# A scheduled attention and FFN kernel: new stage positions, a new VectorE order, and the residual added in one operation

## What is computed

```python
x = x + ln(attention(ln(x), Wq, Wkv, Wo, bo))                  # 32 heads of 16, 8 groups, causal
x = x + ln(ffn0(ln(x)))      # 1792 wide: silu(x gate^T) * (x up^T), then down^T, ternary weights with scales
x = x + ln(lags(ln(x)))      # autocorrelation of each row by FFT, 6 largest lags, softmax of their values,
                             # sum of the row rolled by these lags with these weights
x = x + ln(ffn1(ln(x)))      # 1376 wide, the same form, weights w + b a (rank 16)
```

## Time and profile before

| | us |
|---|---|
| median of 3 runs (lowest 926.63, highest 937.12) | 927.11 |
| the profiled execution, whole | 937.81 |
| its span from the first to the last instruction | 936.0 |
| TensorE busy, all of the span | 755.1 |
| VectorE busy, all of the span | 650.8 |

### The profile page before, as it was taken

How to read it: one execution, slowest core, us unless ns; L and a number is a source line. 1 busy time by engine, 2 the same in 40 slices (tenths; PEclk the granted TensorE clock), 3 DMA queues, 4 the chain that set the end, 5 groups by cost and what they waited for, 6 DMA issues and landing times. The chain is left out here.

```text
span 936.0 us, 15978 instructions
## 1 busy us (share of the span) xinstructions
PE 755.1 (81%) x5102; PEld 409.0 (44%) x5102; DVE 650.8 (70%) x1681; ACT 363.5 (39%) x699; POOL 290.2 (31%) x348
## 2 busy tenths in 40 slices
PE   1966765979898898989859986869974899979995
PEld 1622211222222232222326654646742677757773
DVE  7522874766776767786789977577999954797422
ACT  1112223544565555676003332536431354323221
POOL 3023443112022120233104553334551432533332
PEclk9977755989999998998888997989987999989998
DMA  9499789781231231546556412120229420110100
GB/s 268 82 149 320 232 237 228 148 178 40 43 63 27 48 62 36 136 109 217 175 132 144 83 35 84 62 46 25 61 55 144 85 57 1 23 23 23 46 23 24
DMA packets 144333, 93.12 MB, mean 99 GB/s; under 512 B 111816, under 2 KB 123208, under 8 KB 144056
## 3 DMA queue, kind: packets, MB, share of 16 engines
q1 hardware_dynamic: 133216, 69.93, 33.2%
q10 hardware_dynamic: 10816, 16.91, 6.2%
q0 software_dynamic: 240, 5.51, 2.8%
HBM read 48.20 MB, written 29.04 MB: 83 GB/s over the span
## 5 line engine op out<-in xcount | busy, mean ns | idle before, releaser
L1126 PE MATMUL ps<-arena 128*128 128x256 f16 (+1 forms) x1952 | 236.6, 278 | 26.4 <-issue 13.9
L1126 PEld LDWEIGHTS ps<-arena 128*128 128x128 f16 (+1 forms) x1952 | 195.7, 101 | 70.5 <-issue 24.0
L1353 ACT ACTIVATE arena<-ps 128x1024 f32<-128x1024 f32 (+7 forms) x256 | 163.7, 651 | 124.1 <-PE ps L1383 119.6
L1374 PE MATMUL ps<-arena 96*128 (+4 forms) x384 | 136.8, 382 | 41.8 <-DVE mx L1290 14.2
L1286 DVE CUSTOM_DVE_ANT_0 arena<-ps,arena 128x256 bf16<-128x256 f32 (+3 forms) x256 | 122.2, 489 | 59.0 <-PE ps L1374 50.9
L980 POOL TENSOR_TENSOR arena<-arena 128x256 f32<-128x256 f32 (+1 forms) x100 | 81.2, 812 | 243.2 <-ACT arena L871 241.9
L1148 PE MATMUL ps<-arena 128*128 128x512 f16 (+2 forms) x488 | 123.4, 383 | 17.9 <-POOL arena L986 17.6
L1383 PE MATMUL ps<-arena 99*128 (+4 forms) x384 | 128.3, 352 | 4.7 <-ACT arena L1353 4.3
L1261 POOL TENSOR_SCALAR_AFFINE_SELECT arena<-arena 128x512 f32<-128x512 f32 x64 | 42.1, 659 | 230.6 <-ACT arena L1353 230.3
L1290 DVE TENSOR_REDUCE mx<-ps 128x1 f32<-128x512 f32 x128 | 88.3, 689 | 35.0 <-PE ps L1374 34.2
L1374 PEld LDWEIGHTS ps<-arena 96*128 (+1 forms) x384 | 39.5, 103 | 151.3 <-issue 82.1
(11 more groups left out here) (154 smaller groups left out, 843.0 us busy)
## 6 DMA issues: line engine op xcount, KB each, us to landing
arena<-qp_d SPq DMA_DIRECT2D x48, 128.0 KB, 4.2
lora_d<-arena ACTq DMA_DIRECT2D x20, 256.0 KB, 4.6
arena<-lora_d SPq DMA_DIRECT2D x10, 512.0 KB, 4.8
w1n_d<-arena SPq DMA_DIRECT2D x10, 512.0 KB, 3.3
arena<-rec_d SPq DMA_DIRECT2D x32, 128.0 KB, 2.6
qp_d<-arena SPq DMA_DIRECT2D x12, 256.0 KB, 4.1
w1dn_d<-arena SPq DMA_DIRECT2D x4, 704.0 KB, 3.9
arena<-in_L_ffn_down_w_dram ACTq DMA_DIRECT2D x16, 172.0 KB, 3.7
```

The lines of the kernel that those rows point to most:

```text
L1126: last = nc.tensor.matmul(ps[0:h, b, CH * o:CH * (o + 1)], w(t[0])[:, kt, ht * P:ht * P + h], xt[:, c, t[1], kt, :], start=(kt, t) == (0, ...
L1353: nc.scalar.activation(probs[:, kt % 2, h, kt * P:T], st_bank(h).rearrange("p b n -> p (b n)")[:, kt * P:T], ACT.Exp, scale=HD ** -0.5).th ...
L1374: nc.tensor.matmul(s_bank(g, u)[:, 0:k1 - k0], qt6[0:QROWS, g % RING, h, qt * P:(qt + 1) * P], kt6[0:QROWS, g, k0:k1], start=True, stop=Tr ...
```

## The change

Four things are changed.

1. **The norm.** The first norm's result is no longer written out and added. One `scalar_tensor_tensor` for each tile adds y * rstd to x; the mean that is left out is kept in `shift` for each row, and the last norm adds it. (A norm of x does not see a constant added to a row.) The Newton steps of a 2-column rsqrt are done column by column, two operations for each column and step, without a wait between the columns.
2. **Positions.** The tables become `ROWS_AT` (26, 45, 64, 76), `CORR_AT` (28, 49, 65, 77), `LAGS_AT` (30, 53, 66, 78), `SPEC_AT` (39, 59, 71, 82), `PROD_AT` (43, 61, 73, 84), `BACK_AT` (47, 62, 74, 86). They were (23, 36, 59, 66), (26, 39, 61, 68), (28, 41, 63, 70), (38, 48, 69, 76), (41, 52, 72, 79), (42, 55, 74, 81).
3. **VectorE's order**, with the last attention block behind the first FFN block, hidden tiles 8 to 10 behind the third attention block, and two FFN blocks cut in two around `spectra`. The bias of chunk 3 is loaded again into a buffer of its own (`row_late`).
4. **SyncE's order** and buffers: the prepared tiles have four buffers in place of two, and their stores stand elsewhere.

```diff
+        def rsqrt_by_column(link, n):
+
+            v, r = var[:, 0:n], rstd[:, 0:n]
+            link(nc.vector.tensor_scalar(r.bitcast(I32), v.bitcast(I32), -0.5, float(0x5F3759DF - 0x40000000 - 0x400000), ALU.mult, ALU.add))
+            for _ in range(3):
+
+                for i in range(n):
+                    link.later(nc.vector.tensor_scalar(nw[:, 0, i:i + 1], r[:, i:i + 1], v[:, i:i + 1], r[:, i:i + 1],
+                                                       ALU.mult, ALU.mult))
+                link.settle()
+                for i in range(n):
+                    link.later(nc.vector.tensor_scalar(r[:, i:i + 1], nw[:, 0, i:i + 1], 1.5, r[:, i:i + 1],
+                                                       ALU.add, ALU.mult))
+                link.settle()
...
 -        LAGS_AT = (28, 41, 63, 70)
+        LAGS_AT = (30, 53, 66, 78)
-        BACK_AT = (42, 55, 74, 81)
+        BACK_AT = (47, 62, 74, 86)
...
-        def hidden_store(sp, ht):
+            h, b = height(0, ht), p_of(ht)
+            sp.dma_start(prep_p[b][0:h, :, :], lora_d[:, ht * P:ht * P + h, :].rearrange("m p d -> p m d")).then_inc(prep_loaded[b], 16)
+
+        def hidden_store(sp, ht, then_load=None):
 
             h = height(0, ht)
             sp.wait_ge(prep_done, 2 * (ht + 1))
-            sp.dma_start(w1n_d[:, ht * P:ht * P + h, :].rearrange("i p d -> p i d"), prep_n[ht % 2][0:h, :, :]).then_inc(prep_stored[ht % 2], 16)
-            if ht + 2 < N1:
-                hidden_load(sp, ht + 2)
+            sp.dma_start(w1n_d[:, ht * P:ht * P + h, :].rearrange("i p d -> p i d"), prep_n[ht % 4][0:h, :, :]).then_inc(prep_stored[ht % 4], 16)
+            if then_load:
+                hidden_load(sp, then_load)
...
         def sp_rest(sp):
 
+            transposes(sp, "attn", 0)
+            sp.wait_ge(o_ready, SUB * NCH)
+            sp.dma_start(row_late, bo.rearrange("(a d) -> a d", a=1).broadcast_to([P, D])).then_inc(late_row_loaded, 16)
+            transposes(sp, "attn", 1)
+            transposes(sp, "attn", 2)
+            sp.wait_ge(o_free, SUB * 3)
+            sp.dma_start(row_b[:, :], down_s.rearrange("(a d) -> a d", a=1).broadcast_to([P, D])).then_inc(rows_loaded, 16)
+            hidden_store(sp, 8, 10)
+            hidden_store(sp, 9)
+            hidden_store(sp, 10)
             sp.wait_ge(exps_ready, 1)
             sp.dma_start(pw_d.rearrange("(n p) -> p n", p=P), pw1[:, :], allow_slow_non_contiguous=True).then_inc(pw_stored, 16)
-            sp.wait_ge(pv_done, NT * G)
-            sp.wait_ge(prep_stored[0], 16 * (N1 // 2 + 1))
-            sp.wait_ge(prep_stored[1], 16 * (N1 // 2))
+            for b in range(4):
+                sp.wait_ge(prep_stored[b], 16 * len(range(b, N1, 4)))
             down_load(sp, 0)
             sp.wait_ge(pw_stored, 16)
             sp.dma_start(prep_pw[:, :], pw_d[0:FF1].rearrange("(a n) -> a n", a=1).broadcast_to([P, FF1])).then_inc(pw_loaded, 16)
-            transposes(sp, "attn", 0)
-            sp.dma_start_transpose(w1g[:, 0], w1n_d[0]).then_inc(w1_loaded[0], 16)
-            transposes(sp, "attn", 1)
...
             for i in range(SUB):
                 link.later(nc.vector.bn_aggr(mv[:, i, :], stats[:, i, :]))
             link.settle()
-            link(nc.vector.tensor_scalar(var[:, 0:SUB], mv[:, 0:SUB, 1], LN_EPS, None, ALU.add))
-            rsqrt(link, SUB)
+            link(nc.vector.tensor_scalar(var[:, 0:SUB], mv[:, 0:SUB, 1], LN_EPS, -0.5, ALU.add, ALU.mult))
+            rsqrt_by_column(link, SUB)
...
+        def shifted(link, c, to, first=False):
+
+            was = shift[:, SUB * c:SUB * (c + 1)]
+            link(nc.vector.scalar_tensor_tensor(out=was if first else moved[:, :], in0=mv[:, 0:SUB, 0], scalar=-1.0, in1=rstd[:, 0:SUB],
+                                                op0=ALU.mult, op1=ALU.mult))
+            if not first:
+                link(nc.vector.tensor_tensor(to, was, moved[:, :], ALU.add))
+
...
-        def added(link, c):
-
-            xc = x[:, SUB * c:SUB * (c + 1), :]
-            moments(link)
-            normalised(link, y)
-            link(nc.vector.tensor_tensor(xc, xc, y, ALU.add))
-            row_stats(link, xc)
+        def added(link, c, first=False):
+
+            for i in range(SUB):
+                xi = x[:, SUB * c + i, :]
+                link.later(nc.vector.scalar_tensor_tensor(out=xi, in0=y[:, i, :], scalar=rstd[:, i:i + 1], in1=xi,
+                                                          op0=ALU.mult, op1=ALU.add))
+            shifted(link, c, shift[:, SUB * c:SUB * (c + 1)], first)
+            row_stats(link, x[:, SUB * c:SUB * (c + 1), :])
             moments(link)
             link(nc.vector.tensor_scalar(rstd[:, 0:SUB], rstd[:, 0:SUB], XS, None, ALU.mult))
-            normalised(link, xc)
+
...
-        def after_ffn(dve, link, c):
+        def ffn_added(dve, link, c):
 
             dve.wait_ge(rows_loaded, 32)
             scaled_rows(dve, link, c)
+            moments(link)
             added(link, c)
+
+        def ffn_pieces(dve, link, c):
+
+            normalised_rows(link, c)
             fold(link)
             pieces(dve, link, use_of("ffn", c))
 
+        def after_ffn(dve, link, c):
+
+            ffn_added(dve, link, c)
+            ffn_pieces(dve, link, c)
+
...
             moments(link)
-            normalised(link, y)
+            shifted(link, c, moved[:, :])
+            for i in range(SUB):
+                link.later(nc.vector.tensor_scalar(y[:, i, :], y[:, i, :], rstd[:, i:i + 1], moved[:, i:i + 1], ALU.mult, ALU.add))
+            link.settle()
...
 
         def dve_rest(dve, link):
             dve.wait_ge(rows_loaded, 16)
-            for c in range(NCH):
+            for c in range(3):
                 after_attention(dve, link, c)
+            hidden_tiles(dve, range(8, N1))
+            hidden_scales(dve, link)
             link(nc.vector.memset(notdc[:, :], 1.0))
             link(nc.vector.memset(notdc[0:1, :], 0.0))
             after_ffn(dve, link, 0)
+            dve.wait_ge(late_row_loaded, 16)
+            after_attention(dve, link, 3)
             prepare_down(dve, link, 0)
+            peaks(dve, link, 0)
             prepare_down(dve, link, 1)
-            peaks(dve, link, 0)
+            lag_weights(dve, link, 0)
             after_ffn(dve, link, 1)
-            lag_weights(dve, link, 0)
             spectra(dve, link, 0)
+            prepare_down(dve, link, 2)
+            prepare_down(dve, link, 3)
+            rolled(dve, link, 0)
             peaks(dve, link, 1)
-            prepare_down(dve, link, 2)
             lag_weights(dve, link, 1)
-            rolled(dve, link, 0)
+            ffn_added(dve, link, 2)
             spectra(dve, link, 1)
-            prepare_down(dve, link, 3)
-            after_ffn(dve, link, 2)
+            ffn_pieces(dve, link, 2)
             rolled(dve, link, 1)
-            after_ffn(dve, link, 3)
             peaks(dve, link, 2)
             lag_weights(dve, link, 2)
+            ffn_added(dve, link, 3)
+            spectra(dve, link, 2)
+            ffn_pieces(dve, link, 3)
+            rolled(dve, link, 2)
             peaks(dve, link, 3)
-            spectra(dve, link, 2)
+            last_norm(dve, link, 0)
             lag_weights(dve, link, 3)
-            rolled(dve, link, 2)
             spectra(dve, link, 3)
-            last_norm(dve, link, 0)
             rolled(dve, link, 3)
             for c in range(1, NCH):
                 last_norm(dve, link, c)
...
-            for c in (0, 2, 1):
+            for c in (0, 3, 1):
...
             pe.wait_ge(ctx_stored_last, 16 * REP)
-            for c in range(3):
+            for c in range(2):
                 for i in range(SUB):
                     out_rows(c, i, [ND - 1]).then_inc(o_ready, 1)
             for i in range(SUB):
                 pe.wait_ge(o_free, i + 1)
-                out_rows(3, i, range(ND)).then_inc(o_ready, 1)
+                out_rows(2, i, range(ND)).then_inc(o_ready, 1)
+            for i in range(SUB):
+                out_rows(3, i, [ND - 1]).then_inc(o_ready, 1)
             for i in range(3):
                 pe.wait_ge(w0_loaded[i], 16)
             pe.wait_ge(scales0_ready, N0)
...
-            den_hop(sp, G - 1, 0)
-            den_hop(sp, G - 1, 1)
+            for hop in range(4):
+                den_hop(sp, G - 1, hop)
+            ctx_store(sp, G - 1, 1, ctx_stored_last)
+            hidden_store(sp, 4, 8)
+            hidden_store(sp, 5, 9)
+            hidden_store(sp, 6)
             hidden_store(sp, 7)
-            den_hop(sp, G - 1, 2)
-            den_hop(sp, G - 1, 3)
-            hidden_store(sp, 8)
-            ctx_store(sp, G - 1, 1, ctx_stored_last)
-            hidden_store(sp, 9)
-            hidden_store(sp, 10)
             sp_rest(sp)
 
...
-            hidden_tiles(dve, range(0, 4))
+            hidden_tiles(dve, range(0, 3))
             reciprocals(dve, G - 2)
-            hidden_tiles(dve, range(4, 8))
```

(4 more changed lines are left out.)

109 lines of the change are left out of this document (62 added, 47 removed).

## The result

The changed kernel takes 919.15 us (median of 4 runs, 918.6 to 920.06), the kernel before 928.15 in the same company: a ratio of 0.987, interval 0.983 to 0.991. A later set on one chip gave 921.5 and 930.5, ratio 0.989 (0.985 to 0.993). The executions of the kernel before vary more (926.6 to 937.1) than those of the changed one. So the change gains 9 us where 24 were forecast for the median (from 928 to 904) and 24 for the span (from 936.0 to 912). The profiled execution took 920.06 us, its span is 918.0.

The account below looks back on a forecast made before the run. The last stage was taken as a VectorE-TensorE relay, bound by who waits where: 473.1 + 336.4 blocks + 37.0 waits = 846.5, then to 909.8, span 912 to 913, 23 less; 927.1 - 23 = 904 us, range 886 to 921.

Parts of the forecast that it names:

- 2.4 added for contention: Blocks from the first attention norm to `rolled` 3 run longer as TensorE's gaps shrink by some 15 us: 2.4 us more.
- waits: VectorE's waits from the first attention norm to the end of `rolled` 3 fall from 58.0 to 37.0 us.
- the blocks' sum is then 336.4 us: VectorE's blocks, first attention norm to `rolled` 3: 335.4 + 13.0 moved work - 12.0 arithmetic; fails if off by over 10.
- hidden tiles 8 to 10 and scales: Moved behind the third attention norm, into VectorE's filled stretch: three tiles 12.4 us, with contention and scales 13.
- The pair of one-column operations: In a norm's Newton steps on VectorE, each pair costs 0.25 + 0.03 = 0.28 us, like the bn_aggr pair.
- The old step: Old Newton steps of a norm on VectorE: nine operations at 0.197 us, the norm proper 1.97 us.
- I count as nothing: Ahead of the first attention norm, SyncE no longer puts stores and loads between the last group's hops: no saving counted.
- I carry the difference over: Profiled execution took 937.8 us outside, median 927.1; the 23 us saved in the span was taken off the median: 904.
- Rival 5: One-column pairs in the norms don't overlap, 0.39 us each: 16 us lost, 920 us; chance 0.06.
- Rival 3: Contention in the full stretch may cost each long block another 1 us: + 13, 917, range 909 to 927; chance 0.20.
- Rival 2: Pairs at 0.15 and fewer GpSimd collisions shorten 13 long blocks by 1 us each: 892, range 882 to 893; chance 0.15.
- Rival 4: Slower, 927 to 950: ScalarE's queue blocks at lag terms of tiles 30 and 53, TensorE pays VectorE's delay; chance 0.07.

Follow-up runs that it names:

- undoing the form: The changed kernel with the old three operations over both columns in each Newton step instead of four one-column operations: 915.1 us, ratio 0.983.
- the order alone: The changed positions, VectorE and SyncE order and buffers, with the kernel before's arithmetic (three-operation Newton steps, old residual): 921.6 us, ratio 0.987.
- Experiments 1 and 2: Newton-step forms: changed kernel with three two-column operations 915.1 us, with scalar_tensor_tensor as first one-column pair 925.8, also one two-column second operation 914.0; kernel before with one-column steps 939.0.
- Experiment 3: The changed kernel with GpSimd's second operation of a tile on 2 columns instead of 256 from the third tile on, computing other values: 903.1 us, ratio 0.970.
- the hops alone: The kernel before with SyncE issuing the last group's four hops and context store in a row, stores of hidden tiles 7 to 10 behind them: 939.1 us, ratio 1.010.

## Why the prediction was wrong

The sum was 473.1 + 336.4 + 37.0 = 846.5 for the end of `rolled` 3. The trace has 460.9 + 361.8 + 31.1 = 853.8. The change of each term is best read against the kernel before in its usual execution (930.4 us, span 928.6):

```profile
469.75:859.05 389.30, 323.69 (x2348) 236.58 (x2368) 318.30 (x750) 143.84 (x337) 155.05 (x185) 0.93 0.30 63
```

| | forecast | measured |
|---|---|---|
| start of the first attention norm | 0 | -8.9 |
| blocks (with the 2.4 added for contention) | +3.4 | +23.1 |
| waits | -21.0 | -19.5 |
| behind `rolled` 3 | -6.2 | -5.4 |
| span | -23.8 | -10.6 |

The measured time, 919, lies inside the range of 886 to 921, but by luck: the blocks missed by 20 us, and a front that was counted as nothing gave 9 of them back.

**The step that failed is "the blocks' sum is then 336.4 us".** It was 25 us short (23 with the 2.4 us added later for contention), beyond the 10 the text set as its bound. Against the usual execution (338.6 us) the blocks grew by 23.1. By VectorE's rows, each counted to the start of the next:

| part | forecast | measured |
|---|---|---|
| hidden tiles 8 to 10 and scales | +13.0 | +17.5 |
| 25 norms' Newton steps | -2 | +7.2 |
| residual and shift, 12 blocks | -8 | -6.6 |
| `fold` in the four FFN norms | 0 | +8.9 |
| all else | -2 | -3.9 |

1. *The pair of one-column operations.* Taken as the `bn_aggr` pair, 0.28, "nearest row". It takes 0.49 and 0.37. A `bn_aggr` has no scalar from memory, and the two pairs, which differ in one such scalar an operation, differ by 0.12; that it is the scalar that costs is not shown apart from the form. This is the mis-sized term of the arithmetic: 0.86 a step for a forecast 0.56.
2. *The old step.* Priced at 0.59 from rows of a stretch in which TensorE and GpSimd stood still. Over the whole stretch of the kernel before it averaged 0.76, (18.7 + 16.1 + 14.7 + 7.8) / 75 by these rows, and in the changed order 0.78. That error went the other way, and it is why undoing the form gained 4 us and not 20.

```profile
L228 DVE TENSOR_TENSOR nw<-rstd 128x2 f32<-128x2 f32 x75 | 18.7, 249 | 2.6
L229 DVE SCALAR_TENSOR_TENSOR nw<-nw,var 128x2 f32<-128x2 f32 x75 | 16.1, 215 | 2.6
L231 DVE SCALAR_TENSOR_TENSOR rstd<-nw,rstd 128x2 f32<-128x2 f32 x75 | 14.7, 196 | 2.6
```

3. *Hidden tiles.* 12.4 came from a window beside an idle GpSimd (0.48 us of it busy). In the new place they and the scales take 17.5 us, for 9.9 of which GpSimd is busy.
4. *The folds.* The same operations take 10.4 us before, 19.3 after and 18.2 with the order alone, so it is the place and not the arithmetic. In the third chunk one of them took 0.42 us (first row, the kernel before) and now takes 1.37 beside GpSimd:

```profile
707.33 0.42 DVE L582 TENSOR_TENSOR arena<-arena 128x254 f32<-128x254 f32 x1
...
704.02 2.89 POOL L1046 TENSOR_TENSOR arena<-arena 128x512 f16<-128x512 f32 x2
705.82 1.37 DVE L651 TENSOR_TENSOR arena<-arena 128x254 f32<-128x254 f32 x1
```

The text added 2.4 us of contention for all blocks. The four folds that belong to `lag_weights` became 1.3 us shorter. The sum of all contention did not grow: the excess was 53.7 before, is 45 to 47 after, and 58.2 with the order alone. Experiments 1 and 2 put that down to the one-column steps, which showed no stall. Experiment 3 took only 2.2 us from these folds and 0.3 from the hidden tiles. What remains of their extra time overlaps GpSimd's other instructions, and no run takes those away, so for these two parts contention is read from the overlap.

**Not the step that failed.** The waits came to 31.1 for 37.0: `prepare_down` 1 and 3 2.6 and 7.1 for 2.0 and 5.7, `spectra` 3 7.8 for 8, `rolled` 3 12.0 for 11.5, `spectra` 1 1.7 for 0.3. The two waits of 3.9 ahead of `lag_weights` 1 and 2 did not come back, nor did the 1.7 for tile 10. Of TensorE's gaps those at tiles 30, 53 and 89 were forecast as 9, 9 to 10 and 10 to 12 and are 8.2, 7.7 and 11.1; tile 56 has none, as said; tile 43's was put at 3 and is 6.9, `spectra` 3's at 7 and is 3.8. Not listed were 2.5 us at tile 26 and 4.7 at tile 78. The end behind `rolled` 3 was put at 909.8 - 846.5 = 63.3 us and is 64.2.

**Two further terms, of opposite sign.** What the front could save, "I count as nothing". It gave about 7 us: from the sixth reciprocal to the first attention norm 73.5, 73.5, 70.0 and 73.5 us pass in four profiles with the old front, and 65.5 to 67.2 in eleven with the new. With SyncE's stores between the hops all of it is gone (73.3); but the hops alone, in the kernel before, lose 9 us (82.3), so it belongs to the hops, the buffers and the moved tiles together. The other 2 of the 9 us lie ahead of that point, where single profiles vary by 9 us. And "I carry the difference over" took the waits from an execution 10 us above the median: in the usual one they are 50.6 us, not 58.0, so 7 of the 21 us that the order was to remove weren't there. The waits left over were 6 us smaller than forecast, and these two errors cancel: 19.5 us went for the 21.0 forecast.

**The rivals.** Rival 5 named 920 us, and its 0.39 a pair is near the 0.43 measured. Its mechanism isn't borne out: one operation of L245 takes 0.27 us and the pair 0.45, as the second starts 0.19 behind the first, and undoing the form gave 4 us, not 16. Rival 3 said contention, 917, within 2 us of the result; its place was right in part: folds and hidden tiles together are 13.4 us above the forecast, near its 13. Its growth over all long blocks was not: with the order alone the excess grew by 4.5. Rival 2 fell: the pairs are not 0.15. Rival 4, slower than before, did not decide.

## What to carry to other kernels

Price an operation at its mean over the stretch it will stand in, beside the same neighbours, and not at a row from a pause; and price a new form at the nearest row with the same kind and number of operands, not the same size. In a relay, work moved from beside a wait into the filled stretch costs its full contended price, and the waits that it fills elsewhere must be those of the usual execution. When VectorE's blocks set the end, as in the new order here, less work in them came through for three quarters (12 of 16 us, and 16 to 18 of 21 to 22); then retune the positions, which by themselves gave 6 us here. And beside the median, count from a point that the change does not move: from such a point the order alone is 15 us shorter in its profile, where the median says 9.

## What the runs showed of the hardware

A small VectorE operation (two columns) that collides with GpSimd ends when GpSimd's instruction does: one of 0.16 us takes up to 1.35, and all 57 such cases of the version with three operations end within 0.03 us of a GpSimd end. One-column `tensor_scalar`, `bn_stats` and `bn_aggr` never stretched in any kernel here (the 168 pairs of the changed kernel stay within 0.01 us); a one-column `scalar_tensor_tensor` did in 15 of 84 pairs. So a form that is 46% dearer when quiet (0.86 against 0.59 a step) cost only 10% more in place (0.86 against 0.78). A shorter GpSimd instruction stalls less: with 2 columns instead of 256 the excess in rows that overlap it alone fell from 14.0 to 0.7 us. Why the attention up to the sixth reciprocal takes 394.5 to 403.8 us in single profiles is left open.
